# A four-layer convolution sequence on one core: sixteen shifted copies of the filter tables in DRAM

## The reference

```
x = gamma * softmax(max(qq^T) - qq^T) q + x          # layer 0: q is x as 64 x 65536
x = irfft2(rfft2(x) * rfft2(k1)) [:256,:256] + x*bias[0]   # layer 1: k1[c] = outer(hx[:,c], hy[:,c])
f1 = haar2d(x); acc = sum_i shrink(conv_w[i] @ (f1 * v[i]), tau[i]); x = haar2d_inv(acc) + x   # layer 2
x = irfft2(rfft2(x) * rfft2(k3)) [:256,:256] + x*bias[1]   # layer 3
```

## Time and profile before

| | |
|---|---|
| median of 3 runs | 6840.18 us (6823.84 to 6842.23) |
| the profiled execution | 6835.24 us, its span 6833.4 us |
| PE busy | 6388.9 us, 93% of the span |
| DVE, ACT, POOL busy | 4433.1, 3968.3 and 2698.2 us |
| DMA queue q1 (SP) | 547480 packets, 808.74 MB, 51.3% of 16 engines |
| DMA queue q10 (ACT) | 73728 packets, 134.25 MB, 5.3% |
| chain that ended last | PE 75%, DVE 10%, ACT 8%, DMA 2% |
| loads from `filt` | 2048 of 128 KB, 4.0 us from issue to landing |

### The profile page before, as it was taken

One profiled execution on the slowest core, in us unless ns is written; L12 is line 12 of the kernel. 1 busy time (PEld: TensorE's weight loads), 2 busy tenths in 40 slices (PEclk: granted clock), 3 DMA queues, 4 the chain that ended last, 5 costly groups with the idle time before them and its releaser, 6 DMA issues.

```text
span 6833.4 us, 144168 instructions
## 1 busy us (share of the span) xinstructions
PE 6388.9 (93%) x41056; PEld 5800.8 (85%) x41056; DVE 4433.1 (65%) x7037; ACT 3968.3 (58%) x5913; POOL 2698.2 (39%) x2052
## 2 busy tenths in 40 slices
PE   8998999889998899988999889998899988999689
PEld 7987999779997799977999779997799977998579
DVE  3667646676566764677646776567765677656766
ACT  1568545675456754567545775457654576545865
POOL 0149311483115831167311673117631176311852
PEclk9999999999999999999999999999999999999999
DMA  6654666546664466644666446664466644665236
GB/s 222 126 139 138 123 168 132 141 129 130 169 132 141 126 130 167 132 146 122 131 167 132 147 121 131 167 132 145 122 130 169 131 149 119 131 173 125 80 86 129
DMA packets 621293, 944.27 MB, mean 138 GB/s; under 512 B 62358, under 2 KB 456759, under 8 KB 621208
## 3 DMA queue, kind: packets, MB, share of 16 engines
q1 hardware_dynamic: 547480, 808.74, 51.3%
q10 hardware_dynamic: 73728, 134.25, 5.3%
HBM read 673.92 MB, written 268.83 MB: 138 GB/s over the span
## 4 chain that ended last, share of the span: by engine, by line
PE 75%; DVE 10%; ACT 8%; issue 3%; DMA 2%; POOL 1%; DVEq 1%; SPq 0%; ACTq 0%; POOLq 0%
PE ps L359 26%; PE ps L361 13%; PE ps L387 7%; PE ps L379 7%; PE ps L464 7%; PE ps L416 7%; PE ps L370 6%; DVE work L767 4%; DVE ps L782 4%; ACT ps L601 4%; ACT mag L598 4%; DMA work<-in_x_pix 1%; POOL mag L844 1%; PE ps L337 1%; DMA coef<-work 0%
## 5 line engine op out<-in xcount | busy, mean ns | idle before, releaser
L359 PE MATMUL ps<-work 128*128 128x256 f32 x8192 | 2455.2, 382 | 23.9 <-POOL work L833 16.3
L361 PEld LDWEIGHTS ps<-work 128*128 128x128 f32 x8192 | 1561.8, 191 | 214.3
L361 PE MATMUL ps<-work 128*128 128x128 f32 x8192 | 1578.0, 274 | 0.0
L359 PEld LDWEIGHTS ps<-work 128*128 128x128 f32 x8192 | 1315.8, 192 | 121.5 <-issue 20.7
L833 POOL COPY work<-field 128x512 f32 (+1 forms) x512 | 312.8, 614 | 2308.6 <-DVE ps L731 1623.3
L844 POOL TENSOR_TENSOR mag<-mag,sgn 128x1024 f32<-128x1024 f32 x512 | 1091.8, 2132 | 331.9 <-ACT mag L598 315.6
L862 POOL TENSOR_TENSOR split_a<-field,split_a 128x512 fp32r<-128x512 f32 x512 | 650.8, 1271 | 1418.8 <-ACT split_a L616 1418.8
L782 DVE TENSOR_TENSOR ps<-ps,tau_t 128x1024 f32<-128x1024 f32 x512 | 631.2, 1233 | 313.0 <-ACT ps L601 313.0
L569 ACT ACTIVATE work<-ps 128x512 f32<-128x512 f32 x512 | 306.1, 598 | 874.0 <-PE ps L361 871.1
L616 ACT ACTIVATE split_a<-field 128x512 fp32r (+1 forms) x512 | 322.9, 631 | 698.9 <-PE ps L379 694.6
L767 DVE TENSOR_TENSOR work<-ps,v_t 128x1024 f32<-128x1024 f32 x512 | 622.3, 1215 | 92.9 <-PE ps L464 92.9
(11 more groups left out here) (76 smaller groups left out, 9942.9 us busy)
## 6 DMA issues: line engine op xcount, KB each, us to landing
work<-filt SPq DMA_DIRECT2D x2048, 128.0 KB, 4.0
work<-in_x_pix SPq DMA_DIRECT2D x256, 512.0 KB, 5.4
coef<-work ACTq DMA_DIRECT2D x512, 256.0 KB, 2.1
out<-work SPq DMA_DIRECT2D x512, 256.0 KB, 4.1
rows<-in_x_rows SPq DMA_DIRECT2D x128, 512.0 KB, 4.4
mag<-in_x_rows SPq DMA_DIRECT2D x128, 512.0 KB, 4.4
rows<-coef SPq DMA_DIRECT2D x128, 512.0 KB, 3.6
split_a<-coef SPq DMA_DIRECT2D x64, 512.0 KB, 3.7
```

Of the source, the lines that this page charges most:

```text
L359: nc.tensor.matmul(o_ps, src[:, 0, H * half:H * half + H], tab[:, N - 1::-1], start=True, stop=False)
L361: mm = nc.tensor.matmul(o_ps[:, H:N], src[:, 1, H * half:H * half + H], tab[:, N - 1:H - 1:-1], start=False, stop=True)
```

## The change

`filt` gets a dimension of 16 (`SHIFTS`). Copy s holds 368 elements (`SROW`) of each filter, begun at element s. Sixteen DMAs store them, where one did before, and SP waits for all sixteen. `window` reads for partition p = 16a + s the 256 elements at 16a of copy s, which are the same values as before; the destination of the load is as it was (128 partitions of 256 elements). Every row of the source now starts at a multiple of 64 bytes from the start of `filt`.

```diff
 QROW = N + H
+SHIFTS = 16
+SROW = QROW - SHIFTS
...
-        filt = nc.dram_tensor("filt", (4, C, QROW), F32, kind="Internal").ap()
+        filt = nc.dram_tensor("filt", (4, C, SHIFTS, SROW), F32, kind="Internal").ap()
...
-            row = filt[f, bass.ds(c, 1), :]
-            return bass.AP(row.tensor, row.offset, [[1, H], [1, N]])
+            row = filt[f, bass.ds(c, 1), :, :]
+            return bass.AP(row.tensor, row.offset, [[SHIFTS, H // SHIFTS], [SROW, SHIFTS], [1, N]])
...
-            sp.dma_start(filt.rearrange("f c n -> c f n"), f_out).then_inc(filters_out, 16)
+            for s in range(SHIFTS):
+                sp.dma_start(filt[:, :, s, :].rearrange("f c n -> c f n"), f_out[:, :, s:s + SROW])\
+                    .then_inc(filters_out, 16)
...
-            sp.wait_ge(filters_out, 16)
+            sp.wait_ge(filters_out, 16 * SHIFTS)
```

## The result

| | before | changed |
|---|---|---|
| median of 7 runs | 6829.72 us (6823.84 to 6842.23) | 6851.55 us (6846.90 to 6856.02) |
| ratio | | 1.0029, 95% interval 1.0017 to 1.0041 |
| profiled execution, its span | 6835.24, 6833.4 us | 6856.02, 6854.2 us |

The changed kernel is slower by 21.8 us between the medians: a small loss, clear of noise, and about as large as the 0.3% that the prediction set as the bound of what can be told.

The account below looks back on a forecast made before the run. PE was taken to bound the steady steps, with `filt` loads hidden, so cheaper reads add nothing. Extra stores at the start cost 16.1 less 5.9, 10.2 us, on the median 6840.18: 6850.4 us, range 6832 to 6880.

Parts of the forecast that it names:

- What bounds the kernel: Forward and inverse stages: PE bounds the steps, `filt` loads are hidden with 4.3 and 5.1 us to spare; faster loads gain nothing.
- Sixteen engines or eight: Loads from `filt` in the steady steps: the new pattern's outer dimension puts them on 8 engines, 32 packets a step each.
- the 22 small packets of the 33-row loads: Program's first two loads: 11 completion packets each, taken as 11 engines, the largest number up to 16 dividing 33.
- The price of a read: Loads from `filt` in the steady steps: a packet falls from 116 to 58 ns; landing stays near 4 us.
- the deeper queue: Ground for the 58 ns read: eight loads queued together went at that price, nearest to 32 packets on an engine.
- Rival 1, eight full engines: Steady steps: price stays 116 ns, eight engines are asked for 111%, steps grow, 7304 us; chance 0.10.
- The start: Before the first mixing: fifteen added stores delay row loads by 16.1 us less 5.9 to spare, so mixing starts 10.2 us later.
- 5.9 us to spare: At the start: row load lands by 97.7, but mixing waits for `mix_w` until 103.61.
- The prediction's own sign of being wrong: Start of mixing: first mixing product expected near 114 us; the forecast is wrong if it comes later than 124.
- SP's sixteen issues: At the start: issuing the sixteen stores takes SP 16 x 0.72 = 11.5 us, beside the longer transfer.
- The sum: Whole kernel: the 10.2 us start delay added to the median 6840.18 gives 6850.4 us, +0.15%.
- rival 2: At the start: sixteen stores run at the ports' rate or worse, 26 to 40 us less 5.9, 6860 to 6874; chance 0.12.

Follow-up runs that it names:

- e9: Kernel before with the load's source pattern 8 by 16 by 256, outer step 15 so it can't merge, one copy, eight engines; ratio 1.0001.
- e10: Kernel before with the load's source pattern 4 by 32 by 256, outer step 31 so it can't merge, one copy, four engines; 6842.91 us in one run.
- e1: Kernel before with the load's source pattern written as 8 by 16 by 256, same addresses, one copy; loads stayed on 16 engines; ratio 0.9999.
- e5: Kernel before with the load's source pattern written as 4 by 32 by 256, same addresses, one copy; loads stayed on 16 engines; 6831.24 us.
- e3: Changed kernel with eight copies and stores instead of sixteen, loads on 16 engines; ratio 1.0023.
- e4: Changed kernel with rows of 369 elements instead of 368, so copies start at odd offsets, not multiples of 64 bytes; 6849.38 us.
- e11: Kernel before with filters placed 24576 bytes apart in DRAM instead of 1536, one store and one copy; ratio 1.0008.
- e2: Changed kernel with rows of 384 elements and loads reading copy 0 by the old 128 by 256 pattern, sixteen stores kept; ratio 1.0048.
- e7: Changed kernel with its sixteen stores reading two rows from each of 128 partitions instead of four from each of 64; 6837.17 us.
- e6: Kernel before with source pattern 16 by 8 by 256, eight partitions reading the same row, rows at multiples of 32 bytes, one copy; 6825.87 us.

## Why the prediction came out as it did

- *What bounds the kernel.* Right. PE's steps are 3.98 us in the changed kernel, and reads at 116, 82, 74, 69, 62, 59 and 52 ns a packet all left the steady steps as they were; only with the last, on four engines, did another wait grow.
- *Sixteen engines or eight.* Right, from the 22 small packets of the 33-row loads: the changed kernel's loads show 8 each. e9 and e10 confirm it with 8 and 4. e1 and e5 add that the dimensions must be ones that can't be merged.
- *The price of a read.* 58 ns predicted, 58.6 measured, and the ground given, the deeper queue, was wrong; that the two numbers meet is luck. e9 has the same queue of 32 packets an engine and pays 82; e3 has the queue of before and pays 62. What the runs show is that the price hangs on where the rows lie (one copy, 16 engines: 116 close together, 69 spread) and, for one copy in one small place, falls with the number of engines (116 with 16, 82 with 8, 52 with 4). There the queue on each engine grows as the engines get fewer, so for rows that lie close together the depth isn't ruled out as a part of it. In the earlier trace rows, where a packet cost 58 ns, the eight queued loads were of eight different filters; I took them for a deep queue only, and no run tells the two apart there. Copies, as e4 shows, don't work by alignment; that they work by spreading the rows is what e3 and e11 speak for.
- *Rival 1, eight full engines.* Did not happen, with 2 x 23.6 + 17.2 = 64% of the eight engines busy (65% was predicted). In e10, at 100% of four engines, DVE begins to wait for the stores, but no step grew. A run beyond that wasn't made, so the longer steps of this rival aren't shown to come.
- *The start.* The mechanism was right: stores ahead of the row loads, 5.9 us to spare, the rest on the path. The term that was mis-sized is the price of a store's packet: 67 ns in the sum, 111 measured. With 111 the same sum is 3840 x 111 / 16 = 26.6, less 5.9, 20.7 us; the gap grew by 21.0. The prediction's own sign of being wrong, a first mixing product later than 124, came: it is at 127.58 (3 us of this are the attention products, which ended later in this profile). The step that failed is the reading of the earlier trace rows. A store of 256 packets between row loads and pixel loads went at 70 ns there, 257 GB/s, and I took that as evidence against the port rule of the Trainium skill (SBUF — State Buffer, Door 1: The DMA port swizzle). But the first few microseconds of such stores aren't the rate of a burst. The GB/s of e3 in 40 slices of 94:102, when only its stores are in the queue, from the first ones on, show it:

```profile
GB/s 384 369 376 376 346 361 354 308 346 331 286 263 278 256 241 256 233 196 218 211 203 203 203 218 181 211 211 188 211 226 158 226 196 203 211 196 203 196 211 203
```

It falls from 384 to about 205 in 4 us; in the changed kernel and in e2 the first 2 us with stores go at some 380 GB/s too, with a few packets of pixel loads among them. Why the first microseconds are faster isn't shown. Half of 436 GB/s is not a limit there, neither with the 384 nor with the 257 of the earlier trace rows. The number that the prediction worked out from the Trainium skill (the same section), 26 us of transfer and 20 us of delay, is close to what the burst took.

A second step was wrong and cost nothing: SP's sixteen issues were to take 11.5 us beside the transfer. They took 28.74, the time of the transfer itself (16 x 256 x 111 ns / 16 = 28.4), and in e7, with stores at 67 ns, 17.12 (17.2 by the same sum).
- *The sum.* 6850.4 predicted, 6851.55 measured: a match by luck, in which two errors cancel. The delay was 11 us too small, and the three runs of before, with a median of 6840.18, lay 10.5 us above the median of all seven. The loss in itself was 10.2 predicted and 21.8 measured, twice as much, within the bounds of 8.0 to 34.2 that were given for it. By the prediction's own division, rival 2 (a dearer start, 26 to 40 us of stores) is what happened, to which it gave 0.12.

No version beats the kernel before. Its reads are hidden at 116 ns, so there is nothing for cheaper ones to give back; e11 has most of the cheaper reads without the start, and runs in the same time.

## What to carry to other kernels

Before making a transfer cheaper, see whether anything waits for it: here no wait named the load, so even a price cut by half gave nothing, and the 6 MB of set-up for it stood on the path in front of the first work. A burst of many DMAs in one queue must be priced at its sustained rate, with the partitions that it reads counted, and not from one short DMA of the same kind. When one changes the outer dimension of a DMA's pattern, count the small completion packets in the trace, for they say on how many engines it runs.

## What the runs showed of the hardware

- Reads of overlapping 1 KB rows from one place of 1.5 KB: 116 ns a packet on 16 engines, 82 on 8, 52 on 4 (with 16, 32 and 64 packets a step on each engine). The same reads in three profiles: 116, 118 and 123 ns. With the filters placed 24 KB apart instead of 1.5, 69 ns on 16 engines. Eight partitions reading the very same row: 132 ns.
- All such rows at multiples of 64 bytes, against rows at any multiple of 4: 58.6 and 59 ns (16 copies, 8 engines).
- Sixteen stores in a row, once the burst is under way: 199 GB/s from 64 partitions, 373 GB/s from 128. From 64 partitions the first microseconds go at up to 384 GB/s (e3).
- SP's issue of a load takes 0.33 us with the pattern of one dimension of rows on 16 engines; with the split pattern 0.54 to 0.57 on 16 engines (e3, e6), 0.62 to 0.65 on 8 and 0.55 to 0.59 on 4 (medians). In the burst of sixteen stores an issue takes 1.88 us in the median, about as long as a store's transfer.
